# Two-block FFN kernel on one core: input loads in another order, shared-expert products laid among the last transposes, one semaphore for each row store, and another order at the first gathered tile

## What is computed

```python
w = weights[subjects]; b = bias[subjects]            # per sequence
xt = einsum('bct,bcd->bdt', x, w) + b[:, :, None]    # conditioning of block 1
scores = softmax(xt @ gate_w.T); top_w, top_idx = top_k(scores, 2)
y = sum over the two chosen experts e of  top_w * (silu(xt @ w1[e].T) * (xt @ w3[e].T)) @ w2[e].T
z = silu(xt @ sw1.T) * (xt @ sw3.T) @ sw2.T          # the shared expert, every token
x = x + y + z
H = x @ W.T + s[a] * (x @ A[a].T) @ Bm[a].T          # block 2: one adapter a per sequence
x = x + qdot(gelu(qdot(H, wg0)) * qdot(H, wg1), w_linear)   # fp8 products
```

## Time and profile before

| what | us |
|---|---|
| median of 3 runs (424.0 to 425.26) | 425.01 |
| time of the profiled execution | 424.73 |
| its span, first to last instruction | 422.9 |
| PE busy in it | 411.3 |
| DVE, ACT, POOL busy | 307.1, 248.3, 187.2 |

### The profile page before, as it was taken

How to read it: one execution, slowest core, us unless ns; L and a number is a source line. 1 busy time by engine, 2 the same in 40 slices (tenths; PEclk the granted TensorE clock), 3 DMA queues, 4 the chain that set the end, 5 groups by cost and what they waited for, 6 DMA issues and landing times.

```text
span 422.9 us, 8673 instructions
## 1 busy us (share of the span) xinstructions
PE 411.3 (97%) x2947; PEld 332.5 (79%) x2947; DVE 307.1 (73%) x733; ACT 248.3 (59%) x552; POOL 187.2 (44%) x194
## 2 busy tenths in 40 slices
PE   6989999999899999999999999999999999999996
PEld 5667888888799999999999998885665755757553
DVE  6987978997967666665665654859677786786844
ACT  3996566575255655565566554238466485674854
POOL 1320079501744544554454305637575485755020
PEclk8899999999999999999999999999999999999999
DMA  8999300000356545555655623222232232322111
GB/s 246 377 387 323 96 0 2 1 2 0 90 157 183 159 145 176 157 161 158 170 166 159 138 76 94 82 62 64 82 106 87 64 119 81 101 87 64 50 51 50
DMA packets 37274, 50.44 MB, mean 119 GB/s; under 512 B 4488, under 2 KB 30480, under 8 KB 37232
## 3 DMA queue, kind: packets, MB, share of 16 engines
q1 hardware_dynamic: 29600, 31.53, 22.0%
q0 software_dynamic: 6480, 17.70, 15.7%
q10 hardware_dynamic: 1152, 0.65, 0.7%
HBM read 32.18 MB, written 17.69 MB: 118 GB/s over the span
## 4 chain that ended last, share of the span: by engine, by line
PE 82%; DVE 7%; ACT 4%; DMA 4%; issue 1%; POOL 0%; ACTq 0%; SPq 0%; DVEq 0%
PE bank L1145 16%; PE bank L1147 16%; PE bank L1146 16%; PE bank L1420 13%; PE bank L1435 6%; PE bank L1307 4%; PE bank L1345 2%; PE bank L1346 2%; PE bank L1327 2%; DMA w2raw<-in_rw 2%; PE bank L1386 2%; DMA cst<-in_consts 1%; ACT xtr L466 1%; PE bank L1168 1%; DVE hsl L778 1%
## 5 line engine op out<-in xcount | busy, mean ns | idle before, releaser
L400 POOL DMA_INDIRECT xg<-kept,perm x71 | 68.4, 964 | 92.1 <-PE bank L1307 55.7
L1420 PE MATMUL bank<-h,wg 128*128 128x512 fp8e4 x256 | 61.7, 381 | 0.2 <-ACT ff L643 0.2
L1420 PEld LDWEIGHTS bank<-h,wg 128*128 128x128 fp8e4 x256 | 22.2, 98 | 33.9 <-ACT ff L643 15.0
L1145 PE MATMUL bank<-w13h,xgl 128*128 x142 | 48.7, 343 | 0.0
L976 DVE TENSOR_TENSOR hrl<-bank,hrh 128x256 fp32r<-128x256 f32 (+1 forms) x36 | 15.1, 420 | 45.1 <-ACT hrh L582 45.1
L407 POOL DMA_INDIRECT ga<-slots_out,slot x32 | 32.1, 1004 | 33.3 <-SPq L349 17.4
L1147 PE MATMUL bank<-w13h,xgh 128*128 x142 | 45.8, 322 | 0.0
L1146 PE MATMUL bank<-w13l,xgh 128*128 x142 | 45.8, 322 | 0.0
L641 ACT ACTIVATE gel<-bank 128x512 bf16<-128x512 f32 x64 | 40.4, 631 | 6.4 <-PE bank L1420 3.2
L407 POOL DMA_INDIRECT gb<-slots_out,slot x32 | 38.5, 1202 | 9.8 <-issue 9.8
L643 ACT ACTIVATE ff<-bank 128x512 bf16<-128x512 f32 x64 | 40.9, 639 | 0.0
(11 more groups left out here) (198 smaller groups left out, 1158.4 us busy)
## 6 DMA issues: line engine op xcount, KB each, us to landing
slots_out<-yr SPq DMA_DIRECT2D x35, 256.0 KB, 2.1
xres<-in_x SPq DMA_DIRECT2D x7, 512.0 KB, 10.3
kept<-xtr SPq DMA_DIRECT2D x7, 512.0 KB, 7.0
out_x<-fin SPq DMA_DIRECT2D x7, 512.0 KB, 2.8
w13raw<-in_rw SPq DMA_DIRECT2D x8, 352.0 KB, 4.9
w2raw<-in_rw SPq DMA_DIRECT2D x8, 256.0 KB, 5.8
wgst<-in_wgate SPq DMA_DIRECT2D x16, 128.0 KB, 2.7
xg<-kept,perm POOLq DMA_INDIRECT x71
```

What stands on the lines that cost most here:

```text
L400: pool.indirect_dma_start(out=xg[:, i % 2, j, :], out_offset=None, in_=kept, in_offset=bass.IndirectOffsetOnAxis(perm[:, 2 * i + j:2 * i + ...
L1145: pe.matmul(dst, al, bh, start=first, stop=False, skip_group_check=True)
L1420: ins = pe.matmul(bank[bk][:, :], wg8[:, kk, half, c * P:(c + 1) * P], h8[:, k, kk, :], start=(kk == 0), stop=(kk == KC - 1))
```

## The change

Part by part, in the order of the diff:
- `kept_early` becomes six semaphores, one for each store.
- SP takes over the first part of the constants (third in its queue, ahead of groups 1 to 4) and, behind group 7, their second part and `idi`; ACT issues five loads and not eight.
- SP stores groups 0 to 3, loads experts 0 and 1, and then stores groups 4 to 7.
- `hot_out` is made by POOL and not by DVE.
- POOL, ACT and DVE wait for single stores where each buffer lies over them: ACT for store 1 before the first silu, 3 and 4 before the first high part; DVE for 2 before the first product, 4 and 5 before the first residual.
- ACT converts expert 0's weights before it copies the last group's transposed rows; `shared_act(4)` puts the list scaling between a silu and the high part of the same chunk.
- PE waits for the identity behind `condition(1)`; the last transposes and two routers are laid among parts 0 to 2 of `shared_up(0)`, so `logits(1)` comes behind part 2.
- `perm` comes ahead of half an `add_shared(4)`; at the first gathered pair PE makes two chunks of `shared_down(5)` before the first transposition and one before the second, and DVE adds `shared_down(5)` before the second pair's residual.

```diff
@@
-        kept_early = sem("kept_early")
+        kept_early = [sem(f"kept_early{g}") for g in range(GROUPS - 2)]
@@ SP
             sp.dma_start(xres[:, 0:2, :], x_t[0][:, 0:2, :]).then_inc(x_first[0], 16)
+            sp.dma_start(cst[:, 0:C_BLK], consts[:, 0:C_BLK]).then_inc(s("shapes_in"), 16)
...
             for g in range(5, GROUPS):
                 load_x(g)
-            for g in range(GROUPS - 2):
+            sp.dma_start(cst[:, C_BLK:C_COLS], consts[:, C_BLK:C_COLS]).then_inc(s("const_in"), 16)
+            sp.dma_start(idi[:, :], adapters.partition_broadcast(P)).then_inc(s("ids_in"), 16)
+            for g in range(4):
                 keep(g)
-            for g in range(GROUPS - 2, GROUPS):
-                load_expert(g - GROUPS + 2)
+            load_expert(0)
+            load_expert(1)
+            for g in range(4, GROUPS):
                 keep(g)
@@ POOL
+            pool.wait_ge(s("pick_in"), 16)
+            pool.tensor_scalar(hot_out[:, :], pick[:, 0:BATCH], pick[:, BATCH + CH:BATCH + CH + 1].bitcast(F32),
+                              pick[:, BATCH + CH + 1:].bitcast(F32), ALU.is_equal, ALU.mult).then_inc(s("out_ready"), 1)
             pool.wait_ge(s("gate_in"), 32)
...
-            pool.wait_ge(kept_early, 16 * (GROUPS - 2))
+            for g in range(GROUPS - 2):
+                pool.wait_ge(kept_early[g], 16)
@@ ACT
-            act.dma_start(cst[:, 0:C_BLK], consts[:, 0:C_BLK]).then_inc(s("shapes_in"), 16)
             act.dma_start(gatew[:, :, :], gate).then_inc(s("gate_in"), 16)
-            act.dma_start(cst[:, C_BLK:C_COLS], consts[:, C_BLK:C_COLS]).then_inc(s("const_in"), 16)
             act.dma_start(scl[:, :], scal).then_inc(s("gate_in"), 16)
-            act.dma_start(idi[:, :], adapters.partition_broadcast(P)).then_inc(s("ids_in"), 16)
...
-            keep_xT(GROUPS - 1)
...
                 for c in chunks:
                     shared_silu(i, c, buffers)
+                    if between and c:
+                        token_places(*between[c - 1])
                     shared_h_hi(i, c, buffers)
-                    if between:
-                        token_places(*between[c])
+                if between:
+                    token_places(*between[-1])
...
             routed_weight_hi(0)
-            act.wait_ge(kept_early, 16 * (GROUPS - 2))
+            keep_xT(GROUPS - 1)
+            act.wait_ge(kept_early[1], 16)
             shared_silu(0, 0)
             keep_raw(1)
             routed_weight_hi(1)
+            act.wait_ge(kept_early[3], 16)
+            act.wait_ge(kept_early[4], 16)
             shared_h_hi(0, 0, first=True)
@@ DVE
             weigh_rows(0, GT)
-            dve.wait_ge(s("pick_in"), 16)
-            dve.tensor_scalar(hot_out[:, :], ...)
             add_rows(0, GT)
...
             routed_weight_lo(0)
+            dve.wait_ge(kept_early[2], 16)
             hidden_mul(0, 0)
             shifted(1).then_inc(s("m_sub"), 1)
+            dve.wait_ge(kept_early[4], 16)
+            dve.wait_ge(kept_early[5], 16)
             hidden_lo(0, 0)
...
             hidden_lo(5, 0)
-            add_shared(4, [1])
             dve.wait_ge(s("r_listed"), 1)
             dve.tensor_scalar(perm[:, :], ...).then_inc(s("r_perm"), 1)
+            add_shared(4, [1])
...
             routed_x_lo(0, 0)
+            add_shared(EARLY - 1)
             routed_x_lo(1, 1)
-            add_shared(EARLY - 1)
@@ PE
-            pe.wait_ge(s("shapes_in"), 16)
             for i in range(GROUPS - 1):
                 condition(i + 1)
+                if i == 0:
+                    pe.wait_ge(s("shapes_in"), 16)
                 transpose_xt(i)
...
-            transpose_xt(GROUPS - 1)
             router(GROUPS - 2)
             pe.wait_ge(s("sw_split"), KC)
             shared_up(0, True, parts=[0])
+            transpose_xt(GROUPS - 1)
+            shared_up(0, True, parts=[1])
             router(GROUPS - 1)
-            shared_up(0, True, parts=[1])
+            shared_up(0, True, parts=[2])
             logits(1)
-            shared_up(0, True, parts=range(2, 6))
+            shared_up(0, True, parts=range(3, 6))
...
-            pe.wait_ge(s("h_ready"), EARLY * 3 - 1)
+            shared_down(EARLY - 1, chunks=range(2))
             routed_T(0, 0, True)
-            shared_down(EARLY - 1, chunks=range(2))
-            pe.wait_ge(s("h_ready"), EARLY * 3)
+            shared_down(EARLY - 1, chunks=[2])
             routed_T(1, 1, True)
-            shared_down(EARLY - 1, chunks=[2])
```

More of the change, by code:

```diff
@@ L309, in keep @@
                 sp.wait_ge(s("xt_ready"), g * GT + GT)
-                sp.dma_start(kept_t[g], xtr_of(g)).then_inc(kept_early if g < GROUPS - 2 else kept_late, 16)
+                sp.dma_start(kept_t[g], xtr_of(g)).then_inc(kept_early[g] if g < GROUPS - 2 else kept_late, 16)
             for g in range(1, 5):
@@ L493, in _ @@
                     keep_raw(0)
-            act.wait_ge(s("bias_ready"), 1)
-            act.activation(spare[:, :], bias[:, 0:1], ACT.Silu).then_inc(s("bias_ready"), 1)
-            keep_xT(GROUPS - 1)
             def shared_silu(i, c, buffers=hidden_s):
@@ L523, in routed_weight_hi @@
                 act.activation(w2h[:, i, :], w2raw[:, i, :], ACT.Copy).then_inc(s("rw_hi"), 1)
+            act.wait_ge(s("bias_ready"), 1)
+            act.activation(spare[:, :], bias[:, 0:1], ACT.Silu).then_inc(s("bias_ready"), 1)
             act.wait_ge(s("sw_split"), KC)
@@ L725, in _ @@
             weigh_rows(0, GT)
-            dve.wait_ge(s("pick_in"), 16)
-            dve.tensor_scalar(hot_out[:, :], pick[:, 0:BATCH], pick[:, BATCH + CH:BATCH + CH + 1].bitcast(F32),
-                              pick[:, BATCH + CH + 1:].bitcast(F32), ALU.is_equal, ALU.mult).then_inc(s("out_ready"), 1)
             add_rows(0, GT)
```

## The result

| | before | after |
|---|---|---|
| median of 21 runs each | 424.73 | 423.36 |
| ratio and its 95% interval | | 0.9966 [0.9957, 0.9974] |
| time of the profiled execution | 424.73 | 423.68 |
| its span | 422.9 | 421.9 |

Two later sets of runs of the same changed kernel, each beside runs of the kernel before, gave 422.25 us (0.9947 [0.9927, 0.9967]) and 423.48 us (0.9965 [0.9948, 0.9981]). Faster it is, by 1.4, 2.3 and 1.2 us in the medians of the three sets; the interval of the first is 1.1 to 1.8. The forecast was 0.7 (424.3 from 425.01).

A forecast was written before the change was run, and what follows sets the result against it. PE bounds the kernel, following DVE and ACT at the start and DVE from 34 to 54 us. Terms +0.55 - 0.45 - 0.8 = -0.7 (the start's 0.2 lost) gave a 424.3 us median; 8-in-10 range 422.9 to 425.4.

The forecast's parts named there:

- hot_out leaves DVE: Start: DVE's later rows come 0.26 us earlier, half of it counting at half clock; gain 0.2 (bounds 0 and 0.3).
- rival B: Start: a shorter PE pause lets the clock rise at 11.2, not 14.6; gains 0.8 more, 423.0 us; chance 0.25.
- Loads: Start: moving loads from ACT's queue to SP's is hidden, since condition(1) waits for DVE; cost and gain 0.
- Interleaving: Logits and routing: logits(1) behind one more part delays hidden_lo(0, 0) and DVE's chain; cost 0.55 (bounds 0 and 0.8).
- Single semaphores: Store waits: splitting the wait for six stores gains nothing, and store 5 lands before DVE needs it; 0.
- Rival D: Before hidden_lo(0, 0): DVE waits for store 5, costing 1.8 us if it lands at 38.2; 426.1 us; chance 0.09.
- List scaling: shared_act(4): the silu ahead of the scalings removes PE's wait before shared_up(5); gain 0.45 (bounds 0.3 and 0.5).
- First gathered pair: After shared_up(5): shared_down first covers PE's gather wait; first routed product 0.8 us earlier; gain 0.8 (bounds 0 and 1.3).
- rival C: First gathered pair: pair 2's gather lands over 4 us after issue, and the 0.8 gain goes; 425.1 us; chance 0.13.
- Rival E: Start: POOL's hot_out takes the shared port first, DVE's first product waits up to 0.8 us; 425.1 us; chance 0.08.
- a clock of 1.00 before 14 us: Start: sign that the forecast is wrong because the clock rises earlier than 14.6 and the start gains more.
- a pause where none was: Anywhere in the kernel: sign that the forecast is wrong, a new pause in a place without one before; no size given.

The follow-up runs named there:

- hot_dve: The changed kernel with only hot_out moved back from POOL to DVE; 424.16 us, 0.9987 of the kernel before.
- pair_back: The changed kernel with PE's and DVE's order at the first gathered pair as before, perm still early; 422.01 us, 0.9941 of the kernel before.
- again: The changed kernel run once more, unedited; 422.25 us, 0.9947 of the kernel before.
- weights_behind: The changed kernel with DVE's last weight residual, routed_weight_lo(7), moved behind the first pair's residual; 422.14 us, 0.9936 of the kernel before.
- again_2: The changed kernel unedited, in a later set of runs; 423.48 us, 0.9965 of the kernel before.
- one_wait: The changed kernel with list scaling as before and two waits in all ahead of the first 24 list products; 422.10 us, 0.9935.
- best: The changed kernel without interleaving, with the old order at the first gathered pair, perm early, expert 3's weight residual moved ahead; 421.26 us, 0.9914.

## Why the prediction was right, and where its terms were not

The range of 422.9 to 425.4 held the time, and the gain of 0.34% lies at the bound between no change and faster, a hair on the faster side, which had been given 0.32 against 0.60 for no change. The forecast was 0.9 us too high, of which 0.3 is the median of three runs from which it was counted. That the sum came this near is in part luck: its terms were off by up to 1 us in both directions. By its own steps:

1. **hot_out leaves DVE: gain 0.2. The start gained 0.63.** The 0.28 on DVE was right, condition(1) at 8.87 was not: it began at 9.15. What failed is "0.26 us at half rate are 0.13 at full": the half rate was taken as lying from 7.8 to 14.6 whatever the step did, and here it lay from 6.8 to 12.4, which gave 0.26 by the fourth set. The other 0.37 is the pause in a router of the kernel before, which the prediction did not see (22.89, 0.24 of idle time). The 0.63 is near the 0.8 of rival B, but not by B's way: no shorter pause at 8 us let the clock rise at 11.2. How much of the 0.63 is the step's own stays open (`hot_dve`).
2. **Loads: 0.** Right, by `hot_dve`. (ACT issued eight loads before, not the six that the description of the kernel counts; three of them moved.)
3. **Interleaving: cost 0.55.** Sign and places right (wait at the ranks, 0.32; the logits as what DVE waits for), size 0.2 to 0.4. The logits came at 34.82 where 35.5 was forecast. Of that difference 0.43 is the start's 0.63, of which the term had counted 0.2; the rest is the added part, which cost 1.24 us (34.82 less 34.21 - 0.63) and not 1.49. So the term fell with term 1 for the larger part.
4. **Single semaphores: 0.** Right. DVE shows no idle time at the waits for stores 4 and 5. Rival D did not appear: in DVE's timeline the logits (1.42) are all that it waits for there.
5. **List scaling: gain 0.45. It gained 1.4 in the trace, 1.0 to 1.3 in two pairs of medians.** The pause was priced by its own row, and the products behind it were taken at their length. That is the step that was furthest off, and no bound covered it (0.3 to 0.5). The row that would have told was in the trace of before: 24 products of 72 columns in 1.91 us, 0.08 each, where 12 of the same shape in the next list take 0.56, under 0.05 each.
6. **First gathered pair: gain 0.8. It gained 0.1.** Counted from the end of the first list, the first routed product moved forward by 0.54 of the 0.8 (16.58 us against 17.12) and hidden transposition 0 by 0.08 (19.97 against 20.05). DVE's residual came as reckoned (15.57 behind the list's end, 15.62 before); the first routed product was put at its end, 112.51, but it started at 112.84, since PE made the transposition of pair 1 until 112.68 and stood for another 0.15. The rest is the gather: the prediction let its second transfer start 1.3 us behind the first, and it started 2.49 behind (113.04 - 110.55), because the first issue took 2.19. DVE's products for the hidden transposition were there at 115.81 (115.61 + 0.20), PE began it at 116.23: 0.4 lost, as `pair_back` says too (0.33). That is rival C in its place, with half of its price, but the landing was not what was long: the transposition ran 2.7 us behind the start of the second transfer, inside the 3.3 that were allowed; the issue ahead of it was. The prediction had itself written down, in step 1, that meetings of POOL with a two-input DVE instruction cost, and the row of 1.48 in the earlier trace rows is such a meeting: it starts 0.03 behind a weight subtraction of DVE (106.31).

Rival E's cost did not appear, though its condition was met: `pick` had landed when POOL's hot_out started at 3.22, 0.08 ahead of DVE's first product (3.30). By E the product would have waited; it took 1.25, and POOL's instruction took 1.84 instead. So the order of these two starts did not decide here, and why is not shown (records on POOL are rough). The bias was ready at 5.7, ahead of its first use at 8.0.

Of the signs named for "right", three failed in their times (condition(1) at 8.9: 9.15; the logits near 35.5: 34.82; the residual at 36.4: 35.66), two came (PE's wait at the ranks; no wait for the silu), and the first routed product came half way (0.54 of 0.8). Of those named for "wrong", a clock of 1.00 before 14 us, PE waiting for the gather of pair 2, and a pause where none was all appeared.

So the trace's sum up to hidden transposition 0 is 0.63 - 0.35 + 1.41 + 0.08 = 1.77 of gain: start, logits, lists, first pair. The prediction had -0.55 for the first two together, 0.45 and 0.8. Its errors are thus 0.83, 0.96 and -0.72, and the last hid most of one of the others.

Between that lead of 1.77 and the 1.0 by which the profiled spans differ lies a pause of 0.69 at 120.97 (PE for DVE's product, which came late because ACT's silu did). `again` and `weights_behind` don't have it, `again_2` has 0.52, and `hot_dve` too is slow in this pair (4.61 us from one hidden transposition to the next, 4.74 in the kernel after, 3.86 to 3.96 without the pause). What decides about it was not tried.

## What to carry to other kernels

A pause of the engine that bounds a kernel costs more than its row where many short instructions with waits of their own stand behind it: look at the rate of the instructions behind a pause before pricing it, and put one wait for many in front of such a run. A gather that POOL issues should not fall just behind the start of a DVE subtraction with two SBUF inputs; move the one or the other by a few tenths. Where the start is at half clock, ask how a step may move the slow stretch, not only how it passes through it, and look at several executions, since the stretch moves by itself.

## What was not expected of the hardware

- Fulfilled waits cost time when PE's instructions have no lead: 24 products of 72 columns take 1.83 to 1.91 us with 48 waits behind a pause of 0.3, 0.95 to 0.98 in every kernel without the pause, and 0.95 with the pause and 2 waits. That the lead is what is missing is a reading.
- An indirect transfer's issue on POOL takes 0.94 alone (the first of all 1.17, beside an instruction that reads a bank). When it starts inside a DVE subtraction of two SBUF inputs it takes about as much longer as is left of that: 1.05 to 1.10 with 0.14 to 0.20 left (103.67 and 106.42 in the kernel after), 1.53 to 1.65 with 0.6 to 0.75 left. In most cases it gets through though another such subtraction follows at once (104.76, 106.42, 111.84). At pair 2's first gather in seven profiles (110.55 in the kernel after), started 0.06 to 0.14 into the first of two, it did not, and took 2.17 to 2.23.
- hot_out, 8x128 elements, took 1.84 us on POOL beside DVE's product, and 0.33 on DVE. It costs nothing here, since PE waits for the load of x behind it.
- The clock's record can miss a half-rate stretch: 1.00 was granted from 7.8 to 11.2 by it while the products took 1.51 in place of 0.73.
- A pause of 0.24 to 1.11 us, for which the profile names nothing, stands between the same two products of one router in four of the fourteen profiles, the kernel before among them. It is part of the start's gain as measured here, and its cause is open.
- The steady pairs of the routed stage (31 in the kernel before) take 3.887 us each in six of the fourteen profiles (the kernel before, after, `again_2`, `hot_dve`, `one_wait`, `best`) and 3.860 in the other eight. The same kernel is found in both (`after` and `again`), so it is no property of the edit; over the stage it makes 0.9 us (127.6 against 126.75 from the second hidden transposition to the last). PE is busy throughout in both. What decides between the two is open; whoever compares single profiles of this kernel must take those 0.9 us out first.
